# A fused block of two cross attentions, a mixture of experts and an fp8 layer: the tiles of the routed experts in another order, and the opening steps of the second attention moved in among them

## The chip, the core and the metric

The kernel runs on 1 core of one Trainium2 chip. The metric is the device time in microseconds (us) of one execution. Engines are named as in the profile: PE (TensorE; PEld its weight loads), DVE (VectorE), ACT (ScalarE), POOL (GpSimd), SP (SyncE, which here only issues DMAs).

## What is computed

```python
x = x + L0_xattn(layernorm(x), ctx)          # 16 heads of 64, keys: 77 context rows of each batch
x = x + L0_ffn(layernorm(x))                 # 8 experts, 2 per token, + a shared gated MLP
x = x + L1_xattn(layernorm(x), ctx, ctx)     # unit queries and keys, 16 heads of 16, own layer norm
x = x + L1_ffn(layernorm(x))                 # fp8 quantised linear layer

# L0_ffn
scores = softmax(xf @ gate_w.T);  top_vals, top_idx = top_k(scores, 2)
h = einsum('td,ehd->teh', xf, W1);  y, g = split(h, 2)
z = einsum('te,ted->td', w_dense, einsum('teh,edh->ted', y * silu(g), W2))
z = z + (split of xf @ Ws1.T: y * silu(g)) @ Ws2.T
# L1_xattn
Qp = q @ Wq + bq;  K = l2norm(key @ Wk + bk);  V = key @ Wv + bv;  Q = l2norm(Qp)
out = softmax(Q K^T * 16**-0.5) V @ Wo + bo;  u = out + Qp
return (u - mean(u)) / sqrt(var(u) + 1e-5) * ln_gamma + ln_beta
```

x is 4 x 1024 tokens of 256 floats, all in fp32; the context is 4 x 77 rows of 192. The fp8 layer needs the largest value of all of its input, so it starts only when every token has gone through the second attention.

## The kernel before

There are 4096 tokens in 8 blocks of 512 (4 groups of 128 rows); x stays in on-chip memory (`x_res` in the profile). The program is a row of stages, each a `nc.Block()`: every engine finishes its list of instructions of one stage before any starts the next. Products that need fp32 precision are made of an upper and a lower part of each operand: ACT copies the upper part out, DVE subtracts it from the source for the lower part, and PE does three passes.

**Experts** (`experts`, from line 981; from about 350 us to 642 us of the span). First the 8 blocks go through the shared MLP and the router (`pe_block`, `dve_block`, `act_block`); `dve_route` and `dve_slots` give each of a token's two experts a row in the DRAM tensor `dispatched` (`xd`), where each expert has a region of 4096 rows that is filled in token order; `gp_scatter` (line 1435) writes the normalised rows there with 8 indirect DMAs a block. After the last slots, `dve_list` (line 1355) makes a list of 71 tiles of 128 rows, expert by expert: `expert_no` and `row_no`. Then the 71 tiles are run in a software pipeline: SP's `load` (line 1492) reads the row number and issues the load of a tile, `pe_tile_transpose`, `pe_tile_up`, `pe_tile_hidden` and `pe_tile_down` compute it, `dve_tile_out` (line 1399) copies the result out of PSUM, and SP's `store` (line 1498) writes it back over the same rows. SP's list is in this order: for each i, the load of tile i + 6, then the store of tile i, which waits for the copy of tile i. There are 8 buffers for inputs and 6 for outputs. PE's list in round i is: transpose of tile i + 3, transposes of the hidden part of tile i, up of tile i + 2, down of tile i - 1. At the end DVE and ACT turn the router's scores to weights, `share` (`dve_route_shift`, `dve_route_weights`, lines 1405 to 1426), and SP waits for the last stores (line 1513).

**Second attention** (`attention1`, from line 1653). Its opening: SP issues the loads of the context, Wk, Wv, Wq, Wo and the biases (lines 2414 to 2424); POOL gathers the two expert rows of each token of a block (`gp_gather`, line 2333, 8 indirect DMAs a block); DVE adds them to x (`dve_combine`, line 2120, 2 x 4 instructions), takes the statistics, POOL makes the inverse deviation (`gp_ln`), ACT normalises (`act_normalize`, line 1977); PE transposes, projects queries; keys and values are projected (`pe_project`), the keys are made unit and spread over heads on POOL (`gp_keys`, line 2372), the queries unit (`act_squares`, `gp_root`, `act_unit_queries`), turned and split; then the first scores start (`pe_scores`, line 1884). After that a block of 512 tokens takes 10 chunks of scores, exponentials and values; the next blocks' inputs are prepared beside them: `dve_combine` of block 2 is in `dve_first_block`.

The list of an engine is in the order in which the functions are called in its `@block` section (POOL's for the second attention from line 2436, ACT's from 2474, DVE's from 2555, PE's from 2667).

## Time and profile before

| | us |
|---|---|
| median of 3 runs | 994.44 (992.12 to 996.5) |
| the profiled execution | 993.44, span 991.7 |
| PE busy in the span | 905.3 (91%) |
| DVE busy | 777.0 (78%) |
| ACT busy | 541.8 (55%) |
| POOL busy | 354.5 (36%) |

Times of single instructions are from the start of the span. A stage is read from the place where its chain of waits runs; the busy share of an engine over the whole span is only an average. PEclk in a table by stretches is the TensorE clock that was granted: 1.00 is 2.4 GHz, 0.50 is 1.2 GHz, and what lies between is a stretch with both.

### The profile page before, as it was taken

What the parts mean: (1) busy time and instruction counts of PE and PEld (TensorE: products, weight loads), DVE (VectorE), ACT (ScalarE), POOL (GpSimd) and SP (SyncE); (2) the same over time, 40 slices, a digit from 0 to 9 for tenths busy, and PEclk for the clock granted to TensorE, in tenths of its full rate; (3) what the DMA queues carried; (4) which work ended last, traced back from release to release, by engine and by line L of the source; (5) the groups of instructions that cost most, each with busy time, mean ns of one, the idle gap of its engine ahead of it and who ended that gap; (6) DMA issues with size and microseconds to landing.
All of it is one profiled execution on the core that took longest, in us unless ns stands there. A gap on an engine that the chain in (4) does not pass through costs nothing. (4 is left out here: it accounts for less than half of the span.)

```text
span 991.7 us, 17877 instructions
## 1 busy us (share of the span) xinstructions
PE 905.3 (91%) x5517; PEld 760.3 (77%) x5517; DVE 777.0 (78%) x1843; ACT 541.8 (55%) x1477; POOL 354.5 (36%) x409
## 2 busy tenths in 40 slices
PE   6899999999999999999899999748999999999635
PEld 6899999999999989898799999746655555554324
DVE  7789788788789788887577777766578888867988
ACT  5667577567567555452344444424555655554277
POOL 3243334334334256675400000077446455311330
PEclk9999999999999999999899999966999999999758
DMA  9899950000000033341233334351111011000004
GB/s 309 292 321 319 316 182 0 0 0 1 31 0 2 1 102 128 112 139 64 81 123 123 125 123 123 96 142 49 53 33 38 17 43 43 1 1 0 1 2 168
DMA packets 52760, 91.84 MB, mean 93 GB/s; under 512 B 5351, under 2 KB 27600, under 8 KB 52688
## 3 DMA queue, kind: packets, MB, share of 16 engines
q1 hardware_dynamic: 46544, 74.16, 24.0%
q0 software_dynamic: 6144, 16.79, 5.2%
q8 instruction: 38, 0.62, 0.3%
q14 instruction: 34, 0.28, 0.1%
HBM read 34.56 MB, written 56.36 MB: 92 GB/s over the span
## 5 line engine op out<-in xcount | busy, mean ns | idle before, releaser
L500 POOL TENSOR_TENSOR prob<-prob,row_inv 128x462 f32<-128x462 f32 (+1 forms) x96 | 83.7, 874 | 180.3 <-DVE row_inv L676 180.2
L863 PE MATMUL acc<-u,probT 128*128 128x256 f32 (+1 forms) x960 | 134.0, 288 | 0.9 <-DVE u L688 0.9
L2337 POOL DMA_INDIRECT routed<-dispatched,slots x64 | 65.8, 1028 | 176.4 <-POOLq L1464 158.9
L560 ACT ACTIVATE prob<-score,neg_max 128x77 f32<-128x77 f32 x512 | 120.8, 350 | 14.5 <-DVE neg_max L670 14.3
L816 PE MATMUL score<-m,xnT 128*128 128x462 f32 (+1 forms) x576 | 124.4, 354 | 0.0
L863 PEld LDWEIGHTS acc<-u,probT 128*128 128x128 f32 (+1 forms) x960 | 119.3, 189 | 1.8 <-DVE u L688 1.3
L816 PEld LDWEIGHTS score<-m,xnT 128*128 128x128 f32 x576 | 97.6, 191 | 6.1
L550 ACT ACTIVATE probT<-tr 128x512 fp32r<-128x512 f32 (+1 forms) x96 | 51.9, 543 | 66.3 <-PE tr L802 66.0
L1439 POOL DMA_INDIRECT dispatched<-xn,slots x64 | 69.5, 1087 | 44.7 <-DVEq L1302 27.5
L1893 PE MATMUL score<-qT,kbd 128*128 128x512 f32 (+1 forms) x240 | 79.5, 442 | 0.9 <-DVE qT L2118 0.7
L665 DVE TENSOR_TENSOR probT<-tr,probT 128x512 fp32r<-128x512 f32 (+1 forms) x96 | 56.6, 592 | 12.8 <-ACT probT L550 12.4
L670 DVE TENSOR_REDUCE neg_max<-score 128x6 f32<-128x462 f32 (+1 forms) x96 | 55.7, 580 | 13.1 <-PE score L816 12.7
L1906 PE MATMUL acc<-prob,va 128*102 128x512 f32 x128 | 65.8, 597 | 0.0
L1893 PEld LDWEIGHTS score<-qT,kbd 128*128 128x128 f32 (+1 forms) x240 | 41.6, 190 | 25.8 <-issue 12.8
L674 DVE TENSOR_REDUCE row_sum<-prob 128x6 f32<-128x462 f32 (+1 forms) x96 | 55.4, 577 | 3.5 <-ACT prob L560 2.8
L1991 ACT ACTIVATE prob<-score 128x512 f32<-128x512 f32 (+1 forms) x80 | 45.4, 584 | 14.6 <-PE score L1893 14.6
L802 PE MATMUL tr<-ident,prob 128*128 128x128 f32 x320 | 50.1, 272 | 0.0
L1169 PE MATMUL py<-w1T,wqT 128*128 x216 | 48.1, 359 | 0.0
L1248 ACT ACTIVATE gated<-py 128x192 f32<-128x192 f32 x71 | 23.6, 332 | 42.6 <-PE py L1169 42.6
L1169 PE MATMUL py<-w1T,hidT 128*128 x210 | 46.0, 355 | 0.0
L1392 DVE TENSOR_TENSOR gated<-py,gated 128x192 f32<-128x192 f32 x71 | 25.4, 358 | 23.9 <-ACT gated L1248 23.9
L802 PEld LDWEIGHTS tr<-ident,prob 128*128 128x128 f32 x320 | 38.9, 138 | 4.7 <-DVE probT L665 0.3
(386 smaller groups left out, 2242.9 us busy)
## 6 DMA issues: line engine op xcount, KB each, us to landing
dispatched<-zeros SPq DMA_DIRECT2D x1, 33664.0 KB, 113.1
xn<-dispatched SPq DMA_DIRECT2D x71, 128.0 KB, 2.0
dispatched<-hid SPq DMA_DIRECT2D x71, 128.0 KB, 1.7
out<-x_res SPq DMA_DIRECT2D x7, 512.0 KB, 2.6
x_res<-in_x SPq DMA_DIRECT2D x1, 3072.0 KB, 16.7
consts<-in_L_ffn_W SPq DMA_DIRECT2D x8, 384.0 KB, 3.5
consts<-in_L_ffn_Ws SPq DMA_DIRECT2D x3, 384.0 KB, 4.4
x_res<-in_x SPq DMA_DIRECT2D x2, 512.0 KB, 9.2
```

Source lines behind the costliest of these rows:

```text
L500: gp.tensor_tensor(pr, pr, row_inv[t % 2][:, heads(k)].unsqueeze(2).to_broadcast([P, BANK_HEADS[k], KEYS]), ALU.mult).then_inc(prob_ready, 1)
L560: last = act.activation(prob[t % 2][:, h * KEYS:(h + 1) * KEYS], score_of(t, k)[:, n * KEYS:(n + 1) * KEYS], ACT.Exp, bias=neg_max[t % 2][ ...
L665: dve.tensor_tensor(probT[t % 2][1][:, c0:c0 + n, :], tr_of("p", t, gr)[:, 0:n * P].rearrange("p (c q) -> p c q", q=P), f32(probT[t % 2][0 ...
L670: dve.tensor_reduce(neg_max[t % 2][:, heads(k)], scores_of(t, k), AX_X, ALU.max, negate=True).then_inc(max_ready, 1)
L802: last = pe.transpose(tr_of("p", t, gr)[0:w, (c - c0) * P:(c - c0 + 1) * P], prob[t % 2][:, c * P:c * P + w], g["ident"][:, :])
L816: last = pe.matmul(score_of(t, k)[:, 0:BANK_HEADS[k] * KEYS], xnT[blk][i][:, dc, j * P:(j + 1) * P], m[w][:, dc, cols(k)], start=(n == 0 a ...
L863: last = pe.matmul(acc[t % 2][:, 0:D], probT[t % 2][i][0:rows, c, :], u[k][0:rows, c, :], start=(c == 0 and q == 0), stop=(c == KCH - 1 an ...
L1169: last = pe.matmul(py[i % 2][:, 0:UP], xtT[i % 2][m][:, dc, :], w1[k][:, dc, ds(expert, 1), :].rearrange("p a h -> p (a h)"), start=(q == ...
L1439: gp.indirect_dma_start(out=xd, out_offset=bass.IndirectOffsetOnAxis(ap=g["slots"][:, n, k, j:j + 1], axis=0), in_=xn[n % XN_BUFS][:, j, : ...
L1893: last = pe.matmul(score[c % 2][0:rows, :], keys, qT[n % 2][k][:, f, :], start=(q == 0), stop=(q == 2))
L1906: last = pe.matmul(acc[f][0:A_COLS, :], va[0:rows, b, f, cc, :], p, start=(cc == 0), stop=(cc == A_LAST))
L2337: gp.indirect_dma_start(out=routed[n % 2][:, k, j, :], out_offset=None, in_=xd, in_offset=bass.IndirectOffsetOnAxis(ap=g["slots"][:, n, k, ...
```

## The change

The tile list is ordered by steps: first the first 128 rows of all experts that have any, then the second 128 rows, and so on. It is made with products on PE (`pe_places`, `pe_lists`) and short DVE instructions in the last block, instead of the chain of 13 DVE instructions. In that order, whatever the routing, tokens of block 0 have their results after at most 8 x 512 / 128 = 32 tiles and those of block 1 after 64 (`FIRST_TILES`).

Among the tiles now run: after the store of tile 4, SP issues the seven loads of the second attention's context, Wk, Wv, Wq and three biases (`next_loads`); the router's weights are made in tiles 6 to 11 on DVE, with the exponential on ACT ahead of the tiles; POOL, when the first 32 tiles are stored, gathers block 0's rows (8 indirect DMAs), scales and adds them itself (4 instructions over 128 x 1024), DVE takes the statistics in tiles 50 to 54, POOL the inverse deviation, DVE the shift in tile 57, ACT normalises in tiles 60 to 63; POOL gathers block 1's rows when 64 tiles are stored. The wait for the last stores leaves the end of the stage and goes to the first reader of those rows and the first use of that memory.

The second attention then opens with no input loads but Wo and four rows, with no gather of block 0 or 1, POOL scales and adds block 1's rows (`gp_combine_first`), and the lists of PE, ACT and DVE are reordered: x's transposes and the queries ahead of the values, the unit queries ahead of POOL's work on the keys. Block 2's eight gathers come behind both `gp_keys`. Buffers are placed anew so that these tiles live across both stages.

```diff
+WEIGHTS_AT, NEXT_NORM, NEXT_SHIFT, NEXT_X = 6, 50, 57, 60
+FIRST_TILES = [E * TB * (n + 1) // P for n in range(2)]
...
+        def pe_places(pe):
+            pe.wait_ge(s["used_ready"], 2)
+            pe.wait_ge(s["slot_step"], SLOT_STEPS * LAST + 2)
+            pe.matmul(places.rearrange("p c k -> p (c k)"), earlier[:, :], used[:, :, :].rearrange("p c k -> p (c k)"),
+                      start=True, stop=False, skip_group_check=True)
+            for c in range(LIST_COLS - 1):
+                last = pe.matmul(places[:, c + 1:, :], ones[:, :], used[:, c, :].unsqueeze(1).to_broadcast([P, LIST_COLS - 1 - c, 2]),
+                                 start=False, stop=(c == LIST_COLS - 2), skip_group_check=True)
+            last.then_inc(s["place_mm"], 1)
...
+        def pe_lists(pe):
+            pe.wait_ge(s["at_ready"], LIST_COLS)
+            for i in range(2):
+                for c in range(LIST_COLS):
+                    last = pe.matmul(lists[i], pair_of[:, c, i:i + 1], at_place[:, c, :], start=(c == 0), stop=(c == LIST_COLS - 1), skip_group_check=True)
+            last.then_inc(s["list_mm"], 1)
...
+        def dve_places(dve):
+            dve.wait_ge(s["place_mm"], 1)
+            dve.tensor_copy(place[:, :], places[:, :, 0]).then_inc(s["list_step"], 1)
+            dve.wait_ge(s["list_step"], 7)
+            for c in range(LIST_COLS):
+                dve.tensor_scalar(at_place[:, c, :], tile_no[:, :], place[:, c:c + 1], f32(used[:, c, 0:1]), ALU.is_equal, ALU.mult).then_inc(s["at_ready"], 1)
+
+        def dve_lists(dve):
+            dve.wait_ge(s["list_mm"], 1)
+            dve.tensor_copy(expert_no[:, :], lists[0][:, 0:TILES_B]).then_inc(s["list_ready"], 1)
+            dve.tensor_scalar(row_no[:, :], lists[1][:, 0:TILES_B], float(P), None, ALU.mult).then_inc(s["list_ready"], 1)
...
+        def dve_next_norm(dve, i):
+
+            stats, mean_var = g["stats3"], g["mean_var3"]
+            if i == 0:
+                dve.wait_ge(s["x_added"], TOP_K)
+            if i < TJ:
+                dve.bn_stats(stats[:, i, :], x_tile(0)(i))
+            if i == TJ:
+                dve.drain()
+                for j in range(TJ):
+                    last = dve.bn_aggr(mean_var[:, j, :], stats[:, j, :])
+                last.then_inc(s["x_mv"], 1)
+            if i == NEXT_SHIFT - NEXT_NORM:
+                dve.wait_ge(s["x_rstd"], 1)
+                dve.scalar_tensor_tensor(g["shift3"][:, :], mean_var[:, :, 0], -1.0, g["rstd3"][:, :], ALU.mult, ALU.mult).then_inc(s["x_shift"], 1)
...
+        def act_next_norm(act, j):
+
+            if j == 0:
+                act.wait_ge(s["x_shift"], 1)
+            act.activation(g["xn3"][:, j, :], x_tile(0)(j), ACT.Identity, scale=g["rstd3"][:, j:j + 1], bias=g["shift3"][:, j:j + 1])
...
+        def gp_next_block(gp):
+
+            gp.wait_ge(s["down_mm"], SH_USES)
+            gp_stored(gp, FIRST_TILES[0])
...
+                for j in range(TJ):
+                    gp.indirect_dma_start(out=g["routed"][0][:, k, j, :], out_offset=None, in_=xd,
+                                          in_offset=bass.IndirectOffsetOnAxis(ap=g["slots"][:, 0, k, j:j + 1], axis=0)).then_inc(s["x_gathered"], 16)
+            gp.wait_ge(s["share_ready"], 1)
+            gp.wait_ge(s["x_gathered"], 16 * TOP_K * TJ)
             for k in range(TOP_K):
-                dve.tensor_tensor(g["share"][:, :, k, :], wsum[:, :, k, :], gmax[:, :, :], ALU.mult)
+                part, share = g["routed"][0][:, k, :, :], g["share"][:, 0, k, :].unsqueeze(2).to_broadcast([P, TJ, D])
+                gp.tensor_tensor(part, part, share, ALU.mult).then_inc(s["x_scaled"], 1)
+                gp.wait_ge(s["x_scaled"], k + 1)
+                if k:
+                    gp.wait_ge(s["x_added"], k)
+                gp.tensor_tensor(g["x"][:, 0, :, :], g["x"][:, 0, :, :], part, ALU.add).then_inc(s["x_added"], 1)
+            gp.wait_ge(s["x_mv"], 1)
+            inverse_std(gp, g, g["rstd3"], g["mean_var3"][:, :, 1], s["x_eps"], 1, s["x_rstd"])
+            gp_stored(gp, FIRST_TILES[1])
+            for k in range(TOP_K):
+                for j in range(TJ):
+                    gp.indirect_dma_start(out=g["routed"][1][:, k, j, :], out_offset=None, in_=xd,
+                                          in_offset=bass.IndirectOffsetOnAxis(ap=g["slots"][:, 1, k, j:j + 1], axis=0)).then_inc(g["gathered1"][k], 16)
...
+                NEXT_LOADS = 7
+
+                def next_loads():
+                    sp.wait_ge(s["down_mm"], SH_USES)
+                    sp.dma_start(g["ctxs"][:, :, :], w["ctx_768"].rearrange("b k c -> k b c")).then_inc(s["next_in"], 16)
+                    for dst, src in ((g["wks"], w["L1_xattn_Wk"]), (g["wvs"], w["L1_xattn_Wv"])):
+                        sp.dma_start(dst[:, :, :], src.rearrange("(c p) n -> p c n", p=CP)).then_inc(s["next_in"], 16)
+                    sp.dma_start(g["wqs"][:, :, :], w["L1_xattn_Wq"].rearrange("(c p) n -> p c n", p=P)).then_inc(s["next_in"], 16)
+                    for dst, src in ((g["bk"], w["L1_xattn_bk"]), (g["bv"], w["L1_xattn_bv"]), (g["bq1"][:, :], w["L1_xattn_bq"])):
+                        sp.dma_start(dst, src.partition_broadcast(P)).then_inc(s["next_in"], 16)
...
+                    if i == TILES_B - 1:
+                        sp.wait_ge(s["xT_mm"], TILES_B)
+                        sp.sem_clear(range(xt_in[0].num, xt_in[-1].num + 1))
                     store(i)
-                for k in range(YT_BUFS):
-                    sp.wait_ge(stored[k], 16 * len(range(k, TILES_B, YT_BUFS)))
+                    if i == 4:
+                        next_loads()
+                sp.wait_ge(s["next_in"], 16 * NEXT_LOADS)
...
+                act.wait_ge(s["shifted"], 1)
+                act.activation(logit[:, :, :, :], logit[:, :, :, :], ACT.Exp).then_inc(s["expv_ready"], 1)
...
-                act.wait_ge(s["shifted"], 1)
-                act.activation(logit[:, :, :, :], logit[:, :, :, :], ACT.Exp).then_inc(s["expv_ready"], 1)
+                    if i - NEXT_X in range(TJ):
+                        act_next_norm(act, i - NEXT_X)
...
+                    if i >= WEIGHTS_AT:
+                        dve_route_weights(dve, i - WEIGHTS_AT)
+                    if i >= NEXT_NORM:
+                        dve_next_norm(dve, i - NEXT_NORM)
                 dve_tile_out(dve, TILES_B - 1)
-                dve_route_weights(dve)
...
+        def gp_combine_first(gp, k):
+
+            part, share = routed[1][:, k, :, :], g["share"][:, 1, k, :].unsqueeze(2).to_broadcast([P, TJ, D])
+            gp.wait_ge(g["gathered1"][k], 16 * TJ)
+            gp.tensor_tensor(part, part, share, ALU.mult).then_inc(s["first_scaled"], 1)
+            gp.wait_ge(s["first_scaled"], 2 * k + 1)
+            if k == 0:
+                gp.tensor_tensor(g["x"][:, 1, :, :], g["x"][:, 1, :, :], part, ALU.add).then_inc(s["first_scaled"], 1)
+            else:
+                gp.tensor_tensor(g["x"][:, 1, :, :], g["x"][:, 1, :, :], part, ALU.add).then_inc(s["both_added"], 1)
...
             @block.gpsimd
             def _(gp):
-                gp_gather(gp, 0)
                 gp.memset(vb[:, :, :, :, :], 0.0).then_inc(s["vb_zero"], 1)
-                gp_gather(gp, 1, 0, 4)
-                gp_ln(gp, 0)
+                for k in range(TOP_K):
+                    gp_combine_first(gp, k)
                 gp.wait_ge(s["norm_out"], 1)
                 gp.tensor_tensor(knorm[:, :], knorm[:, :], g["half"][0:KEYS, 0:B], ALU.pow).then_inc(s["norm_pow"], 1)
-                gp_gather(gp, 1, 4)
-                gp_keys(gp, 0, 0)
+                gp_ln(gp, 1)
                 gp_root(gp, 0)
-                gp_keys(gp, 0, 1)
-                gp_gather(gp, 2, 0, 2)
-                gp_ln(gp, 1)
-                gp_gather(gp, 2, 2)
+                for f in range(DC):
+                    gp_keys(gp, 0, f)
+                for k in range(YT_BUFS):
+                    gp.wait_ge(g["stored"][k], 16 * len(range(k, TILES_B, YT_BUFS)))
+                gp_gather(gp, 2)
                 gp.memset(bias_rows[:, :], 0.0).then_inc(fs["rows_set"], 1)
...
+                act_weights(act, 0)
                 for c in range(CC):
                     act_context(act, c)
-                for n in range(3):
-                    act_weights(act, n)
-                for a in range(2):
-                    act_normalize(act, 0, a)
                 for dc in range(DC):
                     act_split(act, 0, 0, dc, xnT)
+                act_weights(act, 1)
+                act_weights(act, 2)
+                for a in range(2):
+                    act_squares(act, 0, a)
                 for f in range(DC):
                     act_keys(act, f)
-                for a in range(2):
-                    act_squares(act, 0, a)
                 act_unit_queries(act, 0)
...
             def _(dve):
+                dve_weights(dve, 0)
                 for c in range(CC):
                     dve_context(dve, c)
-                for n in range(3):
-                    dve_weights(dve, n)
+                for dc in range(DC):
+                    dve_split(dve, 0, 0, dc, xnT)
+                dve_weights(dve, 1)
                 for a in range(2):
                     dve_bias(dve, 0, a)
-                for k in range(TOP_K):
-                    dve_combine(dve, 0, k)
-                dve_stats(dve, 0)
+                dve_weights(dve, 2)
                 dve_key_squares(dve)
-                dve_shift(dve, 0)
                 dve_key_norms(dve)
                 for a in range(2):
-                    dve_bias(dve, 1, a)
+                    dve_queries(dve, 0, a)
                 dve_unit_keys(dve)
-                for dc in range(DC):
-                    dve_split(dve, 0, 0, dc, xnT)
+                dve_stats(dve, 1)
                 dve_row_sums(dve)
                 for f in range(DC):
                     dve_keys(dve, f)
-                dve_combine(dve, 1, 0)
                 for a in range(2):
-                    dve_queries(dve, 0, a)
+                    dve_bias(dve, 1, a)
+                dve_shift(dve, 1)
                 for m in range(C3):
                     dve_value_rows(dve, m)
-                dve_combine(dve, 1, 1)
-                dve_stats(dve, 1)
                 dve_split(dve, 0, 1, 0, qT[0])
                 dve_split(dve, 0, 1, 1, qT[0])
-                dve_shift(dve, 1)
                 dve_query_residual(dve, 0)
...
                 pe_context(pe)
-                for kind in range(2):
-                    for a in range(2):
-                        pe_project(pe, kind, a)
                 for dc in range(DC):
                     pe_transpose_x(pe, 0, dc)
+                for a in range(2):
+                    pe_project(pe, 0, a)
+                for a in range(2):
+                    pe_queries(pe, 0, a)
+                for a in range(2):
+                    pe_project(pe, 1, a)
                 for f in range(DC):
                     pe_turn_keys(pe, f)
-                for a in range(2):
-                    pe_queries(pe, 0, a)
                 for m in range(C3):
                     pe_value_rows(pe, m)
                 for dc in range(DC):
@@ -2750,13 +2896,20 @@
```

## Rows read from the trace of the kernel before

**Rows 1.** table of stretches: busy us of each engine, granted clock, DMA share, GB/s
```profile
500.00:520.00 20.00, 20.00 (x147) 19.93 (x146) 15.15 (x49) 10.09 (x40) 0.00 (x0) 1.00 0.39 120
...
640.00:685.00 45.00, 23.26 (x115) 21.14 (x116) 31.27 (x79) 11.22 (x27) 29.82 (x28) 0.64 0.35 97
```

**Rows 2.** the chain that ended last: start us, us, what
```profile
643.41 0.99 POOL routed L2337
...
658.73 1.69 DVE x_res L2125 x4
...
662.38 1.09 POOL rstd L55
...
678.63 1.04 POOL qinv L2348
...
684.55 4.18 PE score L1893 x9
```

**Rows 3.** SP's instructions in order, the load of tile 11: start us, us
```profile
502.13 0.33 SPq L1496 DMA_DIRECT2D xn<-dispatched  x1
```

**Rows 4.** PE's instructions in order, transposes of tiles 8 and 11
```profile
498.20 0.44 PE L1162 MATMUL tr<-ident,xn 128*128 128x128 f32 x2 [0.41 <-DMA xn<-dispatched]
...
504.49 0.38 PE L1162 MATMUL pgate<-ident,xn 128*128 128x128 f32 x2
```

**Rows 5.** the tile loads of line 1496, from issue to landing
```profile
DMA to landing us min/median/max: 1.8/2.0/3.5
```

**Rows 6.** SP's issues at the head of the second attention
```profile
642.67 0.37 SPq L2414 DMA_DIRECT2D xf<-in_ctx  x1
...
645.88 0.43 SPq L2420 DMA_DIRECT2D bq<-in_L_xattn_bq  x1
```

**Rows 7.** line 2420, the seventh of those loads, to landing
```profile
DMA to landing us min/median/max: 6.5/6.5/6.5
```

**Rows 8.** table of short stretches around the first tiles, columns as in Rows 1
```profile
479.00:481.00 2.00, 0.00 (x0) 0.00 (x0) 1.25 (x2) 0.00 (x0) 1.73 (x5) 1.00 0.26 66
481.00:483.00 2.00, 1.20 (x5) 0.71 (x6) 0.42 (x1) 0.42 (x2) 1.79 (x4) 0.69 0.44 131
...
489.00:491.00 2.00, 2.00 (x15) 1.97 (x15) 1.42 (x6) 0.92 (x4) 0.00 (x0) 1.00 0.00 0
```

**Rows 9.** DVE's instructions at the end of the tiles
```profile
636.51 0.41 DVE L1407 TENSOR_REDUCE gmax<-logit 128x32 f32<-128x256 f32 x1
...
639.86 0.42 DVE L1403 COPY hid<-acc 128x256 f32<-128x256 f32 x1 [0.53 <-PE acc L1189]
...
642.12 0.29 DVE L1426 TENSOR_TENSOR share<-wsum,gmax 128x32 f32<-128x32 f32 x2
```

**Rows 10.** groups of instructions on PE and DVE, 640 to 685 us: busy, mean ns
```profile
L1798 PE MATMUL acc<-qT,kbd 96*77 96x256 f32 x36 | 7.1, 385 | 1.8 <-DVE qT L2059 1.8
L1837 PE MATMUL proj<-wq,xnT 128*128 128x256 f32 x12 | 2.9, 426 | 0.4 <-DVE xnT L2118 0.4
...
L2087 DVE TENSOR_TENSOR xf<-xf,kinv 77x1024 f32<-77x1024 f32 x1 | 1.2, 1222 | 0.0
```

**Rows 11.** a group of POOL over the whole span: sums over 128 x 1024
```profile
L511 POOL TENSOR_TENSOR x_res<-x_res,bo 128x1024 f32 x6 | 14.3, 2389 | 3.9 <-DVE xn L654 3.9
```

**Rows 12.** DVE's and POOL's instructions in order, 671 to 675 us
```profile
671.62 3.41 DVE L2125 SCALAR_TENSOR_TENSOR x_res<-routed,share,x_res 128x256 f32<-128x256 f32 x1
...
672.01 2.72 POOL L2377 TENSOR_TENSOR kbd<-k1T,consts 128x616 fp32r<-128x616 f32 x2
```

**Rows 13.** POOL's last scatter before the tiles, in order
```profile
475.58 0.96 POOL L1439 DMA_INDIRECT dispatched<-xn,slots  x1 [0.30 <-issue]
```

**Rows 14.** ACT's instructions at the head of the experts, in order
```profile
350.96 1.28 ACT L1213 ACT_TABLE_LOAD   x1
352.85 0.60 ACT L1213 ACTIVATE gated<-pg 128x512 f32<-128x512 f32 x1 [0.61 <-PE pg L1128]
```

**Rows 15.** DVE's first sum for block 2, in order
```profile
695.55 1.66 DVE L2125 SCALAR_TENSOR_TENSOR x_res<-routed,share,x_res 128x256 f32<-128x256 f32 x4
```

286 lines of the change are left out of this document (163 added, 123 removed).

## Prediction

> **What bounds the kernel now.** I read the table of stretches first. In the tile stage PE is busy 20.00 us of 20 at the full clock: PE is the bound there. At the head of the second attention, 640 to 685 us, PE is busy 23.26 of 45 us and its clock averages 0.64: nobody is the bound, it is a chain [rows 1]. The chain of waits says which: POOL issues gathers from 643.41, DVE adds block 0's second rows at 658.73, POOL takes up the inverse deviation at 662.38, then normalising, turning and projecting, POOL takes up the queries' root at 678.63, and the first score starts at 684.55 [rows 2]. SP's first instruction of that stage is at 642.67 [rows 6]. So the head lasts 684.55 - 642.67 = 41.9 us, in which block 0's gather and norm stand in front of everything. The change takes them off that chain; what it puts among the tiles must be read against a PE with nothing to spare.
>
> **Blocks and list: 0.** The list's 13 DVE instructions go, and block 7's sums and products can start a microsecond or two earlier. But the first tile load also waits for the last scatter, issued by POOL at 475.58 behind seven others [rows 13], and that is not moved: the cover for anything gained there, and for the few small products and DVE steps that come in. `dve_pairs` adds some 2.5 us to DVE in block 1, where PE is the bound, and POOL makes its constants between scatter 0 and an inverse deviation. I take 0, bounds -0.5 and +1. ACT's functions change once more (exponential ahead of the tiles, silu again, exponential again in attention). The load of a function table takes 1.28 us, and it ran at 350.96 ahead of the wait that its instruction then had to the end [rows 14]; all three new places are in such waits of ACT, so 0; without that cover up to 1.3 us each at two of them.
>
> **The seven loads after tile 4: +7.3.** These stand in SP's queue ahead of the load of tile 11. Issuing them took 645.88 + 0.43 - 642.67 = 3.6 us before [rows 6]. How much slack has a tile load? That of tile 11 was issued at 502.13 [rows 3], lands 2.0 us later by the median [rows 5], and PE turns that tile at 504.49 [rows 4]: 0.36 us of slack. It is not a large buffer although there are 8 tiles of it, because the load of tile i + 7 comes behind the store of tile i, and PE needs it two rounds after that. The trace has a small case: PE waited 0.41 us at 498.20 for a load that landed late [rows 4]. So 3.6 us of issue alone stops PE for 3.3 us. On top the loads themselves are ahead of tile 11 in the DMA engines: they carry 1.28 MB (the sizes in the code), and the seventh took 6.5 us to land before, with gathers beside it [rows 7]; without those, at some 300 GB/s (120 GB/s went at a share of 0.39 [rows 1]), they take 4.3 us behind a first one or two, so I estimate that they are in at about 507.5 and tile 11 at 508.4. PE stops for 3.9 us. Then the clock: PE was idle in 479 to 481, the granted clock fell to half within 481 to 483 and was back at 1.00 in 489 to 491 [rows 8]. A stop of 3.9 us is longer than that one, so I expect the same: nearly 7 us at 1.2 GHz in a stage that is all PE, that is 3.4 us more. Sum 7.3; bounds 3.3 (issue only, clock kept) and 10 (slower landing). Nothing gives it back, since every round after it is PE-bound.
>
> **Other work among the tiles: +0.5.** DVE is busy 15.15 of 20 us, ACT 10.09 [rows 1]: one instruction of about 0.4 us a tile fits in. DVE's products have one source in PSUM and POOL's sums have theirs in SBUF. Block 0's eight gathers move 1 MB beside tile loads that have 0.36 us of slack; a landing later by d costs d - 0.36 every second tile. 0.5, bounds 0 and 2.5. Time is enough for all of it: tile 31 is stored near 565, the eight gathers and four sums on POOL (2.4 us each [rows 11]) end near 590, and DVE takes up the statistics 20 tiles after tile 31. Block 1's gathers start some 12 us before the end of the tiles and take 10.
>
> **End of the tiles: -2.3.** The last copy is at 639.86, and DVE then works on the weights to 642.41 [rows 9], 0.26 before SP starts. All that goes, and so do the two steps from 636.51, of which about 0.5 us reached the end. The last copy ends at 639.8, its store takes 0.4 to issue, 0.2 for the change of stage: 640.4 against 642.67. The wait for the stores to land is no longer there.
>
> **Head of the second attention: 41.9 to 26.3, -15.6.** From the first instruction on: Wk's parts and the context's, 2.7; PE turns the x that is there already, to 3.6; keys, 24 products of 7.1 / 36 = 0.20 us [rows 10], to 8.3; DVE adds the bias and splits Wv, 1.4, squares and sums the keys, 1.2 each (the same size as the row of 1222 ns [rows 10]), to 12.1. The queries take PE 2 x 2.9 meanwhile [rows 10], to 14.0; DVE to 14.7, unit keys to 16.3, block 1's statistics in the 1.8 between the sum and POOL [rows 2], to 18.1. POOL has by then added block 1's rows (1.0 + 4 x 2.4 [rows 11], near 12), and makes the inverse deviation, 2.2, before the queries' root: 20.4. That is a new thing in the way of the queries. From the root to the first score it took 684.55 - 678.63 = 5.9 [rows 2]: 26.3. Bounds: 24.3 if PE stays at full clock, where POOL's sums become the limit, and 31 (rival B).
>
> Of DVE and POOL at once a row speaks: an addition on DVE of 128 x 256 with all sources in SBUF, of which four took 1.69 us elsewhere [rows 2], stretched to 3.41 while POOL did two products lasting 2.72 [rows 12]. The Trainium skill, "SBUF — State Buffer", section "SBUF: two separate sides", says that such a DVE instruction and a POOL instruction exclude each other for the whole of one instruction, whoever starts first. By that each of the three DVE steps under POOL's sums would lose at most one sum, 2.4 us, and half of it would reach the chain; the row shows a wait through two.
>
> **First block: -0.6.** x of block 1 is normalised earlier, so a short wait of PE goes. Block 2's gathers now follow both key products; the first four are in about 9 us after the first score, and DVE wants them 11 us after it (695.55 - 684.55 [rows 15, 2]). The second four arrive about when they are wanted. No loss.
>
> **Sum.** 0 + 7.3 + 0.5 - 2.3 - 15.6 - 0.6 = -10.7 us, from the profiled execution's 993.44 to 982.7. The median of the runs is 1.0 above that execution, so 983.7.
>
> **Rivals.**
> A. The loads cost nothing: a load of a tile can be issued early enough after all, or PE has other work. Against it: 0.36 us of slack, and PE takes its list in order. 983.7 - 7.3 = 976.4.
> B. POOL's four sums starve DVE. If each of DVE's steps with two SBUF sources waits for the whole train, Wq's lower part comes at 12.5, the queries end at 18.4 instead of 14.0, and the first score is at 31: 988.4. For it the 3.41 us; against it that the four sums wait for one another and leave gaps.
> C. Slower: the order of the tiles makes every tile load land later. Neighbours in the list were 128 KB apart in `dispatched` and are now 4 MB apart. A landing later by d costs (d - 0.36) / 2 a tile over 64 loads. From d = 0.36 + 2 x 10.7 / 64 = 0.7 us on the whole gain is gone; the longest landing now is 3.5 [rows 5], and at d = 1.1 the time is 983.7 + 23.7 = 1007. Against it: each load is still one whole piece of 128 KB, as before. The Trainium skill, "DMA: Bandwidth & Descriptors", section "Latency and other measured facts", has rows 4 MiB apart at about half the rate of closer ones; there the distance is between partitions within a copy. No row here shows it, and this rival has its chance from the slack alone.
> D. The moved steps are not ready when wanted (block 1's gathers end late), so that the head still waits: they have some 2 us to spare and 3 us more under the first steps of the head. If it fails by 5 us, 988.7.
>
> **How the numbers follow.** Chances: forecast 0.60, A 0.12, B 0.14, C 0.07, D 0.03, smaller mixtures 0.04. The likeliest is the forecast, 983.7. The unknown costs around it: down to -4 (the clock kept, the loads quick) and -2 (PE at full clock at the head), up to +2.7 (slow landing), +2 (gathers) and +1 (blocks). The range takes in A below and B with half of these costs above, and leaves C out: 976 to 991. A difference of 0.5%, about what a measurement of this kernel can tell from none, is 5 us, so faster means below 989.5: the forecast but for its upper edge, A, and most of B give 0.80; the rest of B and D 0.11 for the same; C and a little more 0.09 for slower.
>
> **What would show it.** After the change: a wait of PE for a tile's load of 3 to 5 us near 505 us, and a granted clock of 0.50 for some 7 us behind it (if absent, A). The landing of tile loads at a median of 2.0 (if 2.5 or more, C). The copies of tile results 2.1 us apart through tiles 31 to 64. The first score 26 us after SP's first instruction of the last stage, with `rstd` and then `qinv` on POOL in its chain; DVE steps of 2 us and more under POOL's sums mean B. And if the first score starts less than 10 us earlier than 684.55 in the span, the sum has failed in its largest terms.

## The result: 11 us slower, not 11 us faster

| | before | after |
|---|---|---|
| median of 6 runs, us | 995.31 (992.12 to 1000.73) | 1006.60 (1002.48 to 1009.38) |
| ratio, 95% interval | | 1.0106 (1.0067 to 1.0144) |
| profiled execution | 993.44 | 1004.65 |

The forecast was 983.7, range 976 to 991: wrong, and the sign with it. Its own last sign of failure came too: the first score starts at 695.57, 11 us later than before and not 10 us or more earlier. The time divided along the trace (us, each value a difference of two starts of instructions):

| | before | after | forecast | measured |
|---|---|---|---|---|
| start of the blocks' products | 349.83 | 348.86 | | -1.0 |
| from there to the first copy of a tile's result | 141.8 | 147.7 | 0 | +5.9 |
| first to last copy (71 tiles) | 148.2 | 170.2 | +7.8 | +22.0 |
| last copy to the first score | 44.7 | 28.8 | -17.9 | -15.9 |
| first score to the end | 307.1 | 307.0 | -0.6 | -0.1 |

So the head, for which the change was made, came nearly as worked out, and the tiles cost more than it gave. A tile takes 2.08 us where nothing is in its way. What the gaps between neighbouring copies had above that, over 0.4 us, in the changed kernel: 6.07 at copy 7; 3.97 and 3.52 at copies 34 and 35; 0.57, 1.11 and 5.02 at copies 65 to 67; single ones of 0.6 to 1.35 besides, which the kernel before has too.

**Copy 7.** SP's DMA issues from the timeline of after (start, duration, engine, line, operation, out<-in), then PE's around the stop (in brackets: idle time before it, and what ended that), then the table by stretches around it.

```profile
504.48 0.33 SPq L1629 DMA_DIRECT2D xn<-dispatched  x1
505.44 0.35 SPq L1633 DMA_DIRECT2D dispatched<-hid  x1
505.85 0.41 SPq L1640 DMA_DIRECT2D xf_early<-in_ctx  x1
...
508.72 0.43 SPq L1645 DMA_DIRECT2D bq<-in_L_xattn_bq  x1
510.08 0.34 SPq L1629 DMA_DIRECT2D xn<-dispatched  x1
```

```profile
508.78 0.27 PE L1246 MATMUL acc<-w2Tb,hidT 128*128 x1
513.60 0.69 PE L1219 MATMUL pgate<-ident,xn 128*128 128x128 f32 x2 [4.54 <-DMA xn<-dispatched]
...
514.36 2.25 PE L1226 MATMUL py<-w1T,hidT 128*128 x6
```

```profile
core 0: us, PE busy (x) PEld busy (x) DVE busy (x) ACT busy (x) POOL busy (x), PEclk, DMA share, GB/s
509.00:511.00 2.00, 0.05 (x1) 0.00 (x0) 0.89 (x3) 0.00 (x0) 0.00 (x0) 1.00 0.96 256
511.00:513.00 2.00, 0.00 (x0) 0.00 (x0) 0.00 (x0) 0.00 (x0) 0.00 (x0) 1.00 0.84 259
513.00:515.00 2.00, 1.40 (x6) 1.37 (x7) 0.26 (x1) 0.64 (x3) 0.00 (x0) 0.51 0.66 199
515.00:517.00 2.00, 2.00 (x11) 2.00 (x10) 0.74 (x3) 0.51 (x3) 0.00 (x0) 0.63 0.01 4
517.00:519.00 2.00, 2.00 (x16) 2.00 (x16) 1.84 (x6) 0.96 (x4) 0.00 (x0) 1.00 0.20 68
```

This is the stop of the forecast: the load behind the seven is issued 5.6 us after the one ahead of them, PE stands for 4.54 us (3.9 forecast), and then works at half the clock for under 4 us, not 7. The gap at this copy was 6.6 to 7.4 us in the six other traces with the loads there and eight buffers.

**Copies 34 and 35.** Two rows of the timeline of POOL, then PE, DVE and ACT in the middle of POOL's eight gathers.

```profile
572.70 1.01 POOL L1542 DMA_INDIRECT routed<-dispatched,slots  x1 [85.98 <-DMA dispatched<-hid]
...
581.50 0.95 POOL L1542 DMA_INDIRECT routed<-dispatched,slots  x1 [0.30 <-issue]
```

```profile
576.38 0.44 PE L1219 MATMUL pgate<-ident,xn 128*128 128x128 f32 x2 [0.37 <-DMA xn<-dispatched]
576.66 0.27 PE L1232 MATMUL pg<-ident,gated 128*128 128x128 f32 x1
...
578.40 0.28 PE L1246 MATMUL acc<-w2Tb,hidT 128*128 x1
```

```profile
579.85 0.42 DVE L1480 COPY hid<-acc 128x256 f32<-128x256 f32 x1 [2.86 <-PE acc L1246]
581.29 0.38 ACT L1301 ACTIVATE hidT<-pgate 128x256 fp32r<-128x256 f32 x1 [4.70 <-remote]
584.09 0.28 ACT L1309 ACTIVATE hidT<-pg 128x128 fp32r<-128x128 f32 x1 [2.42 <-remote]
```

PE's transposes end at 576.82 by the trace; ACT, which waits for nothing else, copies them at 581.29, 4.5 us later. "remote" is how the profile writes that the awaited semaphore was updated just then, and no instruction of it had just ended. PE itself went on to 579.1 and then had to stop for ACT until 582.3, after which its granted clock was 0.50 from 583 to 587: that is in the price of the gap too. I call this a **late report** of PE. It comes again under block 1's gathers (ACT at 660.19 waits 2.44, DVE at 663.02 waits 2.11), and under the scatters of the blocks:

```profile
385.14 0.23 DVE L1327 TENSOR_REDUCE logit<-pgate 128x32 f32<-128x64 f32 x1 [2.68 <-remote]
```

The products that this row waits for had ended at 380.64. The kernel before takes up the same products at 381.15, 0.1 us after their end, under the same scatters. Whether the recording itself has a part in late reports was not tested; the five other times of after (1002.48 to 1009.38) lie around the profiled one.

**The head.** Rows of after that answer to [rows 2], from the chain of waits, and POOL's and DVE's in it:

```profile
671.31 3.84 PE acc L1948 x24
...
676.76 3.35 DVE xf L2221
...
695.57 4.18 PE score L2043 x9
```

```profile
672.59 1.88 DVE L2207 TENSOR_TENSOR wq<-xf_early,wq 128x512 fp32r<-128x512 f32 x1
...
676.69 3.41 DVE L2221 TENSOR_TENSOR xf<-xf 77x1024 f32<-77x1024 f32 x1
...
687.40 1.03 POOL L2507 TENSOR_TENSOR qinv<-ssq,minus_half 128x4 f32<-128x4 f32 x1
```

From SP's first instruction of the stage (668.32) to the first score 27.2 us, forecast 26.3. The squares take 3.41 us beside POOL's sums, where a sum of the same tile without them takes 1.22: rival B to that extent.

### The profile page after: what moved, and what is told of

The parts are those of the page before. It is cut to its first block and busy times, and to the rows that moved or that the text cites. A ratio compares the mean times of both kernels' runs of the same rounds, so it can differ in the third digit from the quotient of the medians.

```text
span 1002.5 us, 17905 instructions
## 1 busy us (share of the span) xinstructions
PE 909.2 (91%) x5526; PEld 762.1 (76%) x5526; DVE 771.5 (77%) x1835; ACT 544.0 (54%) x1479; POOL 368.2 (37%) x418
## 5 line engine op out<-in xcount | busy, mean ns | idle before, releaser
L1226 PE MATMUL py<-w1T,hidT 128*128 x426 | 96.2, 363 | 3.6 <-issue 3.2
L1226 PEld LDWEIGHTS py<-w1T,hidT 128*128 128x128 f32 x426 | 74.7, 198 | 4.3 <-issue 4.2
L697 DVE TENSOR_REDUCE neg_max<-score 128x6 f32<-128x462 f32 (+1 forms) x96 | 55.7, 580 | 11.7 <-PE score L843 11.2
L2485 POOL DMA_INDIRECT routed<-dispatched,slots x48 | 47.9, 998 | 13.3 <-issue 13.3
```

Of the source, the lines that this page charges most:

```text
L697: dve.tensor_reduce(neg_max[t % 2][:, heads(k)], scores_of(t, k), AX_X, ALU.max, negate=True).then_inc(max_ready, 1)
L1226: last = pe.matmul(py[i % 2][:, 0:UP], xtT[i % 2][m][:, dc, :], w1[k][:, dc, ds(expert, 1), :].rearrange("p a h -> p (a h)"), start=(q == ...
```

## The experiments

The kernels of a set ran on the same chip, and each ratio is to the kernel before in that set (the first row is a set of its own; loads_first to gathers_spaced one, the next three with old_kernel_again one, then three, two, and the last with the thirds). "Late reports" says where the trace shows them: "yes" is in the blocks and in the tiles. The other columns are read from the traces as above, in us.

| | ratio (95%) | to first copy | copies | last copy to score | late reports |
|---|---|---|---|---|---|
| after | 1.0106 (1.0067-1.0144) | 147.7 | 170.2 | 28.8 | yes |
| loads_first | 1.0092 (1.0057-1.0127) | 154.9 | 163.8 | 28.7 | yes |
| no_gathers | 0.9975 (0.9947-1.0004) | 149.1 | 159.3 | 27.2 | blocks |
| old_kernel_new_places | 1.0016 (0.9995-1.0038) | 143.4 | 149.4 | 45.1 | blocks |
| gathers_spaced | 1.0075 (1.0050-1.0101) | 154.1 | 162.4 | 28.7 | blocks, block 1's gathers |
| twelve_buffers | 0.9876 (0.9827-0.9926) | 142.5 | 142.2 | 36.2 | no |
| old_twelve_buffers | 0.9901 (0.9867-0.9935) | 140.8 | 142.4 | 43.8 | no |
| constants_later | 0.9991 (0.9968-1.0013) | 140.7 | 158.1 | 35.9 | no |
| changed_again | 1.0104 (1.0068-1.0140) | 145.7 | 167.4 | 28.8 | yes |
| all_but_head | 0.9874 (0.9833-0.9915) | 142.5 | 150.0 | 28.8 | yes |
| block1_in_head | 0.9854 (0.9822-0.9886) | 143.4 | 143.8 | 35.0 | yes |
| plain_on_pool | 0.9979 (0.9953-1.0005) | 144.9 | 158.4 | 30.1 | blocks |
| plain_on_act | 1.0017 (0.9991-1.0043) | 148.9 | 169.2 | 28.5 | blocks |
| norms_before_sums | 0.9840 (0.9803-0.9878) | 141.1 | 142.2 | 34.5 | no |

With one time only (medians of the kernel before beside them 994.85, 992.09, 996.27, 992.09, 992.09): old_kernel_again 988.39, old_kernel_third 993.92, old_kernel_fourth 988.48, old_new_places_again 988.65, changed_third 993.96.

**1. Where the seven loads stand.**

```diff
+                next_loads()
                 sp.wait_ge(s["list_ready"], 2)
 ...
                     store(i)
-                    if i == 4:
-                        next_loads()
```

> The changed kernel with its seven loads issued by SP ahead of the wait for the tile list (where SP has nothing else to do from 477 to 483 us), instead of after the store of tile 4. Theory 1 (the seven loads stop PE once, and the half clock behind it is their price): the one gap of 8.15 us between two copies of tile results near 510 becomes 2.1, so the tile stage is 6 us shorter, less 0 to 2 us for first tile loads that land later beside 1.28 MB: 4 to 6 us below the changed kernel's 1006.6, that is about 1001 to 1002.5. Rival (the stop moves to the start of the tiles with the same length, because the DMA engines are what is short): less than 2 us gained. The two stretches of 8 and 4 us under POOL's sixteen gathers stay in either case.

The gap at copy 7 is gone (copies 6.4 us shorter) and the stage before them 7 us longer, and the ratio is 0.0014 less: under 2 us, as the rival said. But the edit doesn't do what the expectation says. `next_loads` begins with a wait for the last product of the blocks, which stays with it, so the loads did not go out while SP had nothing to do. From the timelines of SP, PE and DVE of loads_first:

```profile
486.47 0.33 SPq L1640 DMA_DIRECT2D xf_early<-in_ctx  x1
...
490.87 3.67 SPq L1629 DMA_DIRECT2D xn<-dispatched  x4
```

```profile
483.10 1.68 PE L1177 MATMUL acc<-ws2T,hidT 128*128 128x256 f32 x12
494.71 0.69 PE L1219 MATMUL tr<-ident,xn 128*128 128x128 f32 x2 [9.93 <-DMA xn<-dispatched]
```

```profile
486.50 0.21 DVE L1461 TENSOR_SCALAR row_no<-pgate 1x71 int32<-1x71 f32 x1
```

The last product ends at 484.8, the first of the seven loads is issued at 486.47 and the list is ready at 486.7, so all seven stand right in front of the tile loads. From the list to the first tile load it is 4.2 us (1.0 in after), and from there to the first copy 14.1 (12.6 in after, 11.2 in changed_again); the rest of the 7 us is later blocks and a late report before the list. Whether loads in SP's idle time would be free was not tried: the memory that they fill is free only after that product.

**2. The gathers left out.** Both trains of indirect DMAs become memsets on POOL.

```diff
-                    gp.indirect_dma_start(out=g["routed"][0][:, k, j, :], ...).then_inc(s["x_gathered"], 16)
+                    gp.memset(g["routed"][0][:, k, j, :], 1.0).then_inc(s["x_gathered"], 16)
```

> The changed kernel in which each of the sixteen gathers of blocks 0 and 1 among the tiles is replaced by a memset on POOL of the same tile (128 x 256) with the same semaphore; it leaves the routed experts' part of blocks 0 and 1 out. POOL's products and sums, the statistics and the norm stay. Theory 1 (the indirect DMAs are what holds up PE's answers to ACT and DVE at 576 to 584 and 654 to 663 us): both stretches go, 7.7 + 4.2 = 12 us off, 994 to 995. Rival (POOL's products and sums, or just the clock): the first stretch stays at 5 us or more, over 1000. A second rival (the delay comes by chance, from this execution): another place shows it.

13 us less by the ratios (of two sets), 11 in the copies, as theory 1 said: no gap over 0.4 us at copies 34 to 36 nor at 65 to 67 but one of 0.68, though the blocks of this trace have late reports and POOL's sums are all there. The gathers, and not POOL's arithmetic, bring the two stretches.

**3. The places of the tiles.**

```diff
-    g["wqT"] = [sb(f"wqT{i}", [P, PAIRS, D], F32R) for i in range(2)]
+    g["wqT"] = [right(f"wqT{i}", [P, PAIRS, D], F32R) for i in range(2)]
 ... (the same for xnT0, xnT1, ws2T)
```

> The kernel before, with nothing changed but where seven of its tiles lie: wqT, xnT0, xnT1 and ws2T at the upper end of on-chip memory as the changed kernel has them, so that w1T and the rest move down. In the trace of the changed kernel PE's results in the block stage reach DVE 1.5 to 4.5 us late under POOL's scatters (the router's logits at 385.14, 400.48, 417.15), in the kernel before never, with the same scatters. Theory 1 (the place of the tiles does it): the blocks become 2 to 3 us longer and the lateness is seen, 997 to 998. Rival (it is the other work in the blocks, or the execution): same as the kernel before within 1 us, no lateness.

Late reports are there (the logits of block 3 wait 1.47 us, of block 4 2.71), and the ratio doesn't tell 0 from 0.3%. Alone it looked like theory 1; experiments 5 and 10 took that back.

**4. The gathers spaced.** On top of loads_first, each of block 0's gathers waits for `y_out` of two tiles more than the one before it.

> As loads_first, and POOL issues block 0's eight gathers one every second tile (each waits for tile 32, 34, ... 46) instead of in one row of 10 us. Theory 1 (the row of eight fills a queue in front of other traffic): a single gather costs nothing measurable, so the stretch of 7.7 us goes: 7 us below loads_first. Rival (each gather costs PE about a microsecond whenever it comes): the same total as loads_first, spread over sixteen tiles. The sums start 22 us later and end near 620, still before the statistics are wanted or up to 3 us behind.

The stretch at copies 33 to 46 falls from 9.0 us (in loads_first) to 1.6, with the first two gathers 1.8 us apart and the rest 4.2 to 4.6: a single list of rows at a time costs nearly nothing. But the expectation of 7 us less is missed: the copies are 1.4 us shorter, the median 2.1. Three us are lost again because POOL's sums end late, which the expectation had as its last point, and other gaps (copies 16 and 28) are 2.6 us longer than in loads_first:

```profile
617.74 0.43 DVE L1516 BATCH_NORM_STATS2 stats<-x_res 128x6 f32<-128x256 f32 x1 [3.11 <-POOL x_res L1553]
```

**5. The kernel before, again.**

> The kernel before, unchanged, once more, for its trace. In the runs so far PE's results reach DVE and ACT 1 to 4.5 us late under POOL's scatters of the block stage: in all four variants, the old kernel with the new places among them, but not in the first trace of the kernel before. Theory 1 (scatters and gathers hold up what PE reports, in either kernel, by chance of the execution or the chip): this trace shows it too, blocks 2 to 6 take 65 to 66 us in place of 63.2. Rival (the places of the tiles do it): no lateness over 0.6 us here.

No late report over 0.6 us, blocks 3 to 6 in 63.1 us: the rival's sign. But the two kernels with the new places in this set, below, have none either.

**6. Twelve buffers.** One number, in the changed kernel and in the kernel before; `xn` has room for twelve tiles in both.

```diff
-XT_BUFS, YT_BUFS = 8, 6
+XT_BUFS, YT_BUFS = 12, 6
```

> The changed kernel with one number changed: 12 buffers for the tiles' inputs instead of 8, so that SP loads ten tiles ahead and not six; the seven loads stay behind the store of tile 4. Theory 1 (the stop at tile 7 is the missing slack of a tile load, 0.36 us): 8 us more slack take all of the 3.6 us of issue and the 4 us of transfer, the gap of 8.15 us becomes 2.1 and the 0.3 to 1.7 us steps that come every 12 us go as well: 10 to 12 us below the changed kernel, 995 to 997. Rival (the DMA engines or PE's clock are what is short, a deeper queue only moves the stop): less than 3 us. The stretches under POOL's gathers stay.

> The kernel before with the same one number changed, 12 for 8. Its trace has eight steps of 0.3 to 1.3 us between copies of tile results, 5.6 us in sum, each some 5 us behind a transfer of 20 KB in the instruction queue, when a tile's load lands late. Theory 1 (missing slack): they go, 4 to 6 us below the kernel before. Rival (they are stops of PE's own instruction stream): no change.

In both traces every copy comes within 2.25 us of the one before, in constants_later of the same set (eight buffers) the gap at copy 7 is 7.0. Of 500 to 520 us in twelve_buffers, the seven loads among it, to be set beside [rows 1]:

```profile
500.00:520.00 20.00, 20.00 (x147) 20.00 (x146) 16.70 (x56) 10.13 (x40) 0.00 (x0) 1.00 0.67 185
```

The slack of a tile's load was the whole price of the seven loads. In the kernel before it was worth 5 to 6 us of the copies by the traces, as theory 1 had it, and 10 by the ratio; the other 4 are not explained. The forecast took the slack as given. In the changed kernel it is 11 us against constants_later; the expectation's 995 to 997 counted from a trace with late reports.

Without late reports the copies end early here, and then the stage's end waits for something else. POOL's first work of the last stage in the timeline, then the instructions of POOL's sequencer at the end of the tile stage (count, duration in ns least/median/longest, first and last start):

```profile
647.60 1.00 POOL L2589 MEMSET vb<- 128x1088 f32 x1 [6.86 <-POOLq L1597]
```

```profile
L1597 POOLq EVENT_SEMAPHORE  x2: 17/17/17, 647.4 to 647.5; - x2
L1597 POOLq DRAIN  x1: 13367/13367/13367, 634.0 to 634.0; - x1
```

DRAIN is an instruction at the end of each engine's list of a stage. The last copy ends at 639.1, POOL's DRAIN at 634.0 + 13.4 = 647.4, which is 6.6 us after the end of POOL's last gather (640.75). In after it is the same 6.6, hidden by the late reports: gather until 661.48, DRAIN until 668.09, last copy 667.21. The gathers are only part of it. Where they are memsets, in no_gathers:

```profile
653.17 2.09 POOL L1557 MEMSET routed<- 128x256 f32 x8 [22.04 <-DMA dispatched<-hid]
```

```profile
L1595 POOLq DRAIN  x1: 7239/7239/7239, 653.3 to 653.3; - x1
```

The memsets end at 655.26, the DRAIN at 660.59, 5.3 us later. It is 5.3 us too behind POOL's last instruction in the kernel before (484.48, DRAIN until 489.81) and in plain_on_act (635.28 and 640.60), 6.0 in the two kernels that gather block 1's rows in the next stage, and 6.6 behind the plain DMAs of plain_on_pool. So whatever POOL does last keeps the stage open for 5 to 7 us more; a DMA adds about one.

**7. The list's small work later.** POOL's iotas and copies go from behind scatter 0 to behind scatter 5, `dve_pairs` from block 1 to block 5, `gp_constants` behind `list_ready`.

```diff
-            if n == 1:
+            if n == LAST - 2:
                 dve.wait_ge(s["const_out"], 5)
                 dve_pairs(dve)
 ...
+                gp.wait_ge(s["list_ready"], 2)
                 gp_constants(gp)
```

> The changed kernel with the small work of the new list moved: POOL's iotas and copies from behind scatter 0 to behind scatter 5, DVE's dve_pairs from block 1 to block 5, and POOL's constants of the second attention behind the list. Theory 1 (they cost the 2.5 to 3 us that blocks 1 and 2 are longer than before, 34.7 us against 31.5, and keep DVE from the list at 477 to 482 us by sharing its port to on-chip memory with POOL): blocks 1 and 2 together 31.5 to 32, and the first tile load 19 to 20 us after block 7's first product instead of 21.5: 3 to 5 us below the changed kernel, 1001.5 to 1003.5. Rival (the late reports of PE do it, whatever POOL and DVE do besides): within 1 us of it.

Blocks 1 and 2 take 31.5 us, in the kernel before 31.6, in all traces of the changed kernel with that work in its old place 33.5 to 34.9 (33.5 without late reports): that is the edit's own gain, 2 us without late reports and 3 with them. The part for the list brought nothing: the first tile load is issued 19.0 to 19.1 us after block 7's first product here, and in changed_third and twelve_buffers too; the 21.6 of after, from which the expectation counted, was of that trace. The first copy comes 140.7 us after the blocks' start, as in the kernel before. The set has no late reports, so the expected 1001.5 to 1003.5 can't be held against its 993.37.

**8. The changed kernel again, and the edits put together.** all_but_head is twelve buffers, constants_later, and block 0's gathers one a tile; block1_in_head moves block 1's gathers to the head of POOL's list of the last stage, the key norms in between block 1's two sums, and its statistics and inverse deviation further back.

> The changed kernel, unchanged, beside the kernel before once more. So far the traces are of two kinds: in some executions what PE reports reaches ACT and DVE 1 to 4.5 us late under POOL's scatters and gathers (the changed kernel's own trace, all four of one set of runs, the old kernel with new places among them), in others never (the kernel before twice, and all three variants run beside its second time). Theory 1 (this belongs to the execution, and the changed kernel pays for it only where it gathers among the tiles): if this trace shows no lateness, the stretches under the gathers cost 2 us instead of 12, but the stage then ends with POOL's DRAIN, which in all traces ends 6.65 us after the last gather was issued, so 7 to 8 us of the gain are lost again, and the time is 996 to 1000 (ratio 1.001 to 1.005); if it shows lateness, 1004 to 1008 (ratio 1.009 to 1.013). Rival (the lateness is a property of the changed kernel's code): lateness here whatever the others show.

> The changed kernel with three edits together: 12 buffers for tile inputs, the list's small work moved to block 5 and POOL's later constants behind the list (as in constants_later), and block 0's eight gathers one a tile (each waits for the copy of tile 31, 32, ... 38). Block 1's gathers as in the changed kernel. Expected from the single ones: no step over 0.5 us between copies through tile 63, blocks 1 and 2 together 31.5 us, and POOL's DRAIN still holding the stage's end until 6.65 us after the last gather's issue, so 35 to 36 us from the last copy to the first score: 979 to 981. Rival (the gains overlap): as twelve_buffers, 982.6.

> As all_but_head, and block 1's eight gathers are issued by POOL as its first work of the last stage, not among the tiles, with POOL's order then: first sum of block 1, key norms, second sum, root of the queries, spread keys, inverse deviation of block 1; DVE takes block 1's statistics behind the value rows. Theory 1 (what holds the end of the tile stage is POOL's DRAIN behind its gathers): SP's first instruction of the last stage comes 1.1 us after the last copy's end instead of 8.4, the head from there takes 29 instead of 27.2 us: 5 to 6 us below all_but_head, 974 to 976. Rival (another engine holds the stage's end, or the head grows by the gathers' 10 us): same as all_but_head or slower.

changed_again repeats the result within 0.0002, with late reports. all_but_head came as its rival: 982.41, and by the ratio as twelve_buffers (0.9874 and 0.9876), which was in a set without late reports. The gathers of block 0 were not one a tile throughout: the first four go out 1.3 us apart, since their tiles had been copied before POOL came to them, the other four 1.6 to 2.6. They cost one gap of 2.0 us, of which the next three give 1.2 back; block 1's, in a train, cost 1.1 and 3.7 us at copies 66 and 67. block1_in_head loses those (its one gap is 2.7 us, at copy 35). SP's first instruction of the last stage stands 0.8 us behind the last copy's end, and POOL's DRAIN is over long before:

```profile
636.55 1.28 SPq L1629 DMA_DIRECT2D dispatched<-hid  x2
638.28 0.40 SPq L2571 DMA_DIRECT2D wo1f<-in_L_xattn_Wo  x1
```

But the head is 33.7 us from there, not 29: its chain now begins with the eight gathers and one sum ahead of the key norms (654.60). So 2 us by the ratios instead of 5 to 6.

**9. What in a gather it is.** The same sixteen transfers, without lists of rows.

```diff
-                    gp.indirect_dma_start(out=g["routed"][0][:, k, j, :], out_offset=None, in_=xd, in_offset=...)
+                    gp.dma_start(g["routed"][0][:, k, j, :], xd[(k * TJ + j) * REGION:(k * TJ + j) * REGION + P, :])
```

> The changed kernel in which the sixteen gathers among the tiles are plain DMAs on the same queue (POOL), at the same places, of the same size (128 rows of 1 KB into the same tiles), each from one whole piece of dispatched instead of by a list of rows; it leaves the routed experts' right rows of blocks 0 and 1 out. Theory 1 (any train of DMAs that POOL issues holds up PE's reports): if the blocks of this trace show late reports (they keep their indirect scatters), so do tiles 33 to 37 and 65 to 67, at 4 us and more a step: ratio about 1.010. Theory 2 (the list of rows does it: 128 pieces of 1 KB by address): no steps there, ratio 0.998.

> As plain_on_pool, but ACT issues the sixteen DMAs from its own queue, behind tiles 33 and 65, in two trains of eight. Theory 1 (it is POOL's way of issuing): no late reports in the tiles even where the blocks show them, only ACT's own time for eight issues (8 x 0.4 = 3 us a train) in the way of PE: two steps of 1 to 3 us, and no DRAIN behind the last one. Theory 2 (it is the traffic of 1 MB beside the tile loads, whoever issues it): steps of 4 us as in the changed kernel, plus ACT's.

In plain_on_pool the blocks' scatters have late reports, the tiles have none:

```profile
385.59 0.23 DVE L1327 TENSOR_REDUCE logit<-pgate 128x32 f32<-128x64 f32 x1 [2.80 <-remote]
...
571.99 3.76 POOL L1542 DMA_DIRECT2D routed<-dispatched  x7
```

Copies 34 to 36 have gaps of 0.2, 0.6 and 1.4 us over 2.08, and PE's clock stays at 1.00. So neither the megabyte of traffic nor POOL's queue does it, but the transfers by lists of rows in a train. Three things differ between the two at once: the list, the place of the rows in DRAM (one piece here), and the pace, since the eight plain DMAs go out in 4 us and the gathers in 10; which of them it is stays open. From ACT's queue the same transfers cost 5 us a train, ACT's own issuing:

```profile
583.63 3.08 ACTq L1720 DMA_DIRECT2D routed<-dispatched  x5
586.76 0.38 ACT L1301 ACTIVATE hidT<-pgate 128x256 fp32r<-128x256 f32 x1 [5.27 <-issue]
```

**10. Chip or places.**

> The kernel before, unchanged, for its trace beside the changed kernel's on the same chip. The late reports of PE have been seen in 8 traces, all of kernels with the new places of wqT, xnT0, xnT1 and ws2T, and not in the 3 traces with the old places nor in 2 with the new. Theory 1 (they belong to the chip or the execution): if changed_third shows them in the blocks, this one does too. Rival (they need the new places, and the chip only decides how often): this one shows none, while old_new_places_again and changed_third do.

> The kernel before with only the four tiles' places changed, once more, between the other two on the same chip. Theory 1 (chip or execution): as old_kernel_third, whatever that shows. Rival (the places): late reports of the router's logits by 1 us or more in blocks 3 to 7 here, none in old_kernel_third.

> The changed kernel once more, as the sign of which kind this chip is. With late reports: steps of 4 and 3 us at copies 34 and 35, the first score 28 us after the last copy, as in its first two traces. Without them: steps under 1 us there, and the first score 35 to 36 us after the last copy, because POOL's DRAIN then ends 8 us after the last copy.

> The kernel before, unchanged, on whatever chip this is. Late reports of PE came in all runs of some sets (4 of 4, 3 of 3, 2 of 2) and in none of others (0 of 4, 0 of 4), so they go with the chip or the hour, and the new places alone do not bring them (5 traces with new places and none late). Open is whether the old places are spared on a chip that has them. If this trace shows the router's logits late by 1 us or more in blocks 2 to 7, they are not; if it shows none, it stays open, since the chip may be of the other kind.

None of the four has a late report; chip 15 is that of old_kernel_fourth and of experiments 5 to 7, and had none either time. changed_third came as its second case: copies 34 to 36 with 1.2 us in sum, first score 35.8 us after the last copy, its DRAIN until 658.6 where the last copy ended at 650.7; its one time is 993.96 in a set where the kernel before has a median of 992.09. A single time says little: old_kernel_fourth's 988.48 stands beside one of 996.27 for the same kernel. Over all sets, late reports were in every trace of three sets (4, 3 and 2 traces) and in none of the others (4, 4 and 1), so they go with the chip or the hour. The new places alone don't bring them: five traces have those places and none late. What stays **open**: no trace of the kernel before is known to come from a set that shows them, so whether the old places are spared is not shown. One comparison speaks against it. With late reports old_kernel_new_places has its first copy 4.4 us later than old_new_places_again has it without, but beside the kernel before of its own set it is only 1.6 us slower (0.5 less to 3.8 more). Not known is also where between PE and the waiting engine a report is held.

**11. The key norms first.**

```diff
-                gp_combine_first(gp, 0)
                 gp.wait_ge(s["norm_out"], 1)
                 gp.tensor_tensor(knorm[:, :], knorm[:, :], ..., ALU.pow).then_inc(s["norm_pow"], 1)
+                gp_combine_first(gp, 0)
                 gp_combine_first(gp, 1)
```

> block1_in_head with one POOL instruction moved: the square root of the key norms ahead of the first sum of block 1 instead of behind it. In block1_in_head the chain of the head runs through POOL's gathers (to 649.35), the first sum, and the key norms at 654.60, which DVE has waited for since 651.4. Theory: the key chain starts 3 us earlier, and the first score with it, less what the sums then wait: 2 to 3 us below block1_in_head, ratio 0.982 to 0.984. Rival (the root of the queries or the spread keys behind both sums are the bound): no change.

The fastest of all, 975.62 us (974.05 to 977.05, 4 runs), 0.984 of the kernel before (0.9803 to 0.9878). The number came as expected, but in a set without late reports, and its interval takes in the 0.9854 of block1_in_head. From the stage's start to the score it is 33.2 us against 33.7, not 3 us less: what the keys gained they lose again beside the sums. From its chain, the product of the unit keys, 1.22 us in after, and twice four copies of constants, which the same chain of after has at 0.35 and 0.31 us for four:

```profile
649.87 3.22 DVE xf L2231
653.08 2.08 DVE va L2240 x4
655.16 2.46 DVE vb L2243 x4
```

## Why the prediction was wrong, step by step

- **Blocks and list, 0 (bounds -0.5 and +1): wrong, +5.9 in the profiled execution.** The step said that the small products and DVE steps are covered. Of the 5.9, 3.4 are there before block 7's first product and 2.4 between it and the first tile load. 2 to 3 us are the small work's own (experiment 7). I named POOL's constants and `dve_pairs`, and gave them no price because PE is the bound there; but PE's next products wait for what DVE and POOL do. The rest is late reports under the scatters, and in this trace an instruction of the list:

```profile
477.42 4.17 DVE L1456 TENSOR_SCALAR at_place<-tile_no,place,used 128x72 fp32r<-128x72 f32 x3
```

  The three take 0.8 us in eleven other traces of the changed kernel and its variants, and 4.2 once more, in plain_on_act. In both slow ones the last of the three, begun 0.15 us into POOL's last scatter, ends with POOL's first pause behind that scatter, eight memsets and a select: POOL's select ends at 481.54 in after and 485.79 in plain_on_act, DVE's instruction at 481.59 and 485.85. What held it was not tried.
- **Seven loads, +7.3: right, +6.1.** In six other traces it was 6.6 to 7.4. The stop was 4.5 for 3.9, the clock's share 1.5 for 3.4. A stop of 4.5 us brought less than 4 us at half clock here, where [rows 8] had about 7 behind a shorter one. What I missed is that the slack was a choice: four buffers more, in memory that is there, make it 0.
- **Other work among the tiles, +0.5 (0 to 2.5): the step that failed.** It cost 14.4 us, 7.7 under block 0's gathers and 6.7 under block 1's (with the 6.1 of the loads that is 20.5 of the 22.0 by which the copies grew; the other 1.5 are not assigned). The sum asked how late a tile's load would land beside 1 MB of gathers; the median landing stayed at 2.0 us (of the nine of 71 landings that this trace tells, and of 62 in changed_third). It did not ask what else a train of gathers holds up, and the kernel before had no row of it: its gathers stand where PE waits anyway, its scatters showed nothing in its trace. A gap in the rows was read as a price near nothing, where the bound above should have been a whole train, about 10 us each. On a chip without late reports the same gathers cost 1.2 us at copies 34 to 36 (changed_third).
- **End of tiles, -2.3: -1.3, and by luck.** "The wait for the stores to land is no longer there" was right; that the stage ends for every engine only when POOL's DRAIN is over, 6.6 us after block 1's last gather, was not seen. Where PE's reports are prompt, it costs 7 to 8 us (twelve_buffers, constants_later, changed_third). So block 1's gathers are paid in any case, in the tiles or at the end.
- **Head, 26.3: 27.2.** Right, rival B included at a fifth of its price. The first block, -0.6: -0.1.
- **The rivals.** A (loads for nothing) is false here, true with twelve buffers. C (the order of the tiles) is false: landing 2.0 us, as before, and no steady lateness of the copies; rows of `dispatched` 4 MB apart between neighbouring transfers cost nothing that a row shows, and the rule of the Trainium skill cited there, "DMA: Bandwidth & Descriptors", section "Latency and other measured facts", is about distances within a copy. D (the head waits for moved steps) is false in after; in the traces without late reports its effect came, 7.5 us, by another mechanism, the DRAIN, and without being late data. It had 0.03. The forecast took from the Trainium skill, "SBUF — State Buffer", section "SBUF: two separate sides", that a DVE instruction loses at most one of POOL's: 3.41 us again, where 1.22 plus one sum of 2.4 would be 3.6. The trace agrees with that here; the row in the forecast, through two of POOL's products, doesn't.

The range failed for the same reason as the sign: no bound in it stood for "everything that a new kind of traffic in a stage with a full PE can hold up", though the text said of that stage that PE has nothing to spare.

## What to carry to other kernels

Before work is moved from a chain into a stage whose bound engine is full, count how late each input of that stage may be; if it is 0.4 us, first make it 8 (here: 8 to 12 buffers, 1.0% for the kernel before alone, against 0.5 to 0.6% more for the whole change with the edits of experiments 7, 8 and 11, by ratios of different sets whose intervals overlap). Trains of indirect DMAs do not belong beside a chain of short instructions between engines: spread them to one in about four microseconds, and check their real distance in the trace. Keep POOL's last work of a stage, DMA or not, some 7 us clear of the stage's end, since POOL's DRAIN counts there. And an operation that the trace shows only where nobody waits for anything has no price yet: bound it by its whole length.
